# A masked 4,096-key cross-attention: half of the mask moved from TensorE to a product on GpSimd

## The reference, cut to what matters

```python
energy = jnp.einsum('nqhd,nkhd->nhqk', q, k)
energy = jnp.where(mask == 0, jnp.float32(-1e+20), energy)
attn = jax.nn.softmax(energy / math.sqrt(EMBED), axis=3)
out = jnp.einsum('nhql,nlhd->nqhd', attn, v).reshape(N, q_len, HEADS * HEAD_DIM)
return out @ w_out.T + b_out
```

## Time and profile before

| what | us |
|---|---|
| median of 3 runs | 945.77 |
| the runs | 946.16, 945.77, 938.29 |
| span of the profiled execution | 937.9 |
| the run nearest to it | 938.29 |
| PE busy | 915.0 |
| DVE busy | 592.0 |
| ACT busy | 446.4 |
| POOL busy | 101.3 |

### The profile page before, as it was taken

How to read it: one execution, slowest core, us unless ns; L and a number is a source line. 1 busy time by engine, 2 the same in 40 slices (tenths; PEclk the granted TensorE clock), 3 DMA queues, 4 the chain that set the end, 5 groups by cost and what they waited for, 6 DMA issues and landing times.

```text
span 937.9 us, 20632 instructions
## 1 busy us (share of the span) xinstructions
PE 915.0 (98%) x7488; PEld 542.7 (58%) x7490; DVE 592.0 (63%) x1546; ACT 446.4 (48%) x835; POOL 101.3 (11%) x138
## 2 busy tenths in 40 slices
PE   8999999999999999899999999999999999999998
PEld 8888886557666556544444444444444444467656
DVE  3455445655332226777777877777777777558884
ACT  3444434541121224666666666666666666642110
POOL 1222221000600110100000000000000000003000
PEclk9999999999999999999999999999999999999999
DMA  7944598608117217993564455446545543710201
GB/s 252 298 171 168 178 384 286 201 2 272 57 31 118 79 48 197 280 211 63 69 85 71 61 77 81 66 61 83 75 62 71 83 65 82 137 45 1 46 24 45
DMA packets 78391, 109.88 MB, mean 117 GB/s; under 512 B 27036, under 2 KB 64544, under 8 KB 74307
## 3 DMA queue, kind: packets, MB, share of 16 engines
q1 hardware_dynamic: 73019, 93.70, 45.7%
q0 software_dynamic: 4960, 14.96, 4.3%
q10 hardware_dynamic: 360, 0.50, 0.2%
HBM read 86.29 MB, written 21.06 MB: 114 GB/s over the span
## 4 chain that ended last, share of the span: by engine, by line
PE 87%; DVE 5%; SPq 2%; DMA 2%; ACT 1%; issue 1%; ACTq 0%; POOL 0%; DVEq 0%
PE bank L1486 15%; PE bank L1507 13%; PE bank L1495 9%; PE bank L1464 7%; PE bank L1343 6%; PE bank L1137 5%; PE bank L1124 4%; PE bank L1371 3%; PE bank L1717 2%; PE bank L1090 2%; PE bank L1311 2%; PE bank L1229 1%; PE bank L1220 1%; PE bank L1777 1%; SPq L486 1%
## 5 line engine op out<-in xcount | busy, mean ns | idle before, releaser
L986 ACT ACTIVATE region<-bank 128x512 f32<-128x512 f32 x512 | 277.9, 595 | 152.0 <-PE bank L1495 152.0
L2192 DVE CUSTOM_DVE_ANT_0 xnT<-bank,region 128x1024 bf16<-128x1024 f32 x128 | 156.1, 1220 | 79.9 <-issue 79.8
L1486 PE MATMUL bank<-region 128*128 (+1 forms) x1024 | 158.1, 276 | 2.1 <-ACT region L986 1.4
L2192 DVE CUSTOM_DVE_ANT_0 region<-bank,region 128x1024 bf16<-128x1024 f32 x128 | 156.3, 1221 | 0.4
L1507 PE MATMUL bank<-region 128*32 128x256 f32 x2048 | 138.9, 385 | 0.0
L1486 PEld LDWEIGHTS bank<-region 128*128 128x128 bf16 x1024 | 69.5, 98 | 119.9 <-issue 59.8
L1495 PE MATMUL bank<-region,identb 64*64 64x512 bf16 x1024 | 105.2, 401 | 0.0
L1507 PEld LDWEIGHTS bank<-region 128*32 128x32 f32 x2048 | 58.9, 109 | 40.5 <-ACT region L986 14.5
L1464 PE MATMUL bank<-region,xnT 64*128 64x512 bf16 x248 | 75.1, 382 | 1.1 <-DVE region L2192 1.1
L1466 PE MATMUL bank<-region,xnT 64*128 64x512 bf16 x248 | 75.1, 382 | 0.0
L741 POOL COPY region<-region 128x512 f32<-128x512 f32 x30 | 18.4, 613 | 389.7 <-PE bank L1507 389.7
(11 more groups left out here) (384 smaller groups left out, 1228.1 us busy)
## 6 DMA issues: line engine op xcount, KB each, us to landing
region<-keys_split SPq DMA_DIRECT2D x224, 128.0 KB, 4.9
region<-in_ctx SPq DMA_DIRECT2D x32, 512.0 KB, 7.6
keys_split<-region POOLq DMA_DIRECT2D x48, 256.0 KB, 4.4
region<-in_L_ffn_we_gate SPq DMA_DIRECT2D x8, 688.0 KB
region<-in_L_ffn_we_up SPq DMA_DIRECT2D x8, 688.0 KB
region<-in_mask_1x1xSxS_ik SPq DMA_DIRECT2D x1, 4096.0 KB, 16.4
region<-in_L_ffn_we_down SPq DMA_DIRECT2D x8, 512.0 KB
mask_kept<-region SPq DMA_DIRECT2D x1, 2048.0 KB, 10.9
```

The source lines that it names most:

```text
L986: nc.scalar.activation(prob4[n % PROBS].rearrange("p a b -> p (a b)"), bank[:, SCORE4[n], :], ACT.Exp, scale=SCALE4).then_inc(exp4_ready, 1)
L1486: mm(bank[:, SCORE4[n], k * S:(k + 1) * S], slab[s][:, t * P:(t + 1) * P], qT4[:, bass.ds(u, 1), :].rearrange("p o q -> p (o q)"), start=( ...
L2192: v.tensor_tensor_reduce(out=junk[q], in0=bank[:, 3 + 2 * q:5 + 2 * q, :].rearrange("p a b -> p (a b)"), in1=maskN[:, q, 2 * c * CH:2 * (c ...
```

## The change

Of the eight groups of a unit, the even ones (POOLED = 0, 2, 4, 6) have no mask matmuls any more: their score4 is raised by the second score matmul. ACT takes the exponential of the unmasked scores. GpSimd then multiplies the 32 bits of each exponential, read as an integer, by an integer 0 or 1 (keep4), in place, one instruction of 128 x 512 for each half, so eight more in a unit, and raises probs_kept, for which values_group of these groups waits instead of exp4_ready. The copy of the values comes behind the second of the eight, and in the last unit the inverse root is in that place. The odd groups stay as they are; maskT holds only theirs.

keep4 is made in stage 2 by two ACT instructions per pooled group in place of one. The constant for masked becomes -2^67. Queries whose whole row is masked are handled apart: in stage 1 DVE also reduces each piece of the mask to its maximum (eight tensor_reduce) and, in chunks 11 to 14, subtracts the row's result (eight tensor_scalar); where a row is wholly masked, the variance of the norm before stage 4 is replaced by a huge one (floor in layer_stats, two small instructions changed). The mask's store to DRAM waits for chunk 14 instead of 10. wout and woutT lie in the first key slab, so wout is loaded when that slab has been used for the last time, behind unit 28's scores, ahead of the loads for stage 5 on SP, and its four transposes and ACT's copy stand in front of o4_T(0) in the last unit instead of behind stage 1.

```diff
+POOLED = (0, 2, 4, 6)
+ON_PE = [g for g in range(GROUPS) if g not in POOLED]
-MASKED = -float((np.float32(1e20).view(np.uint32) & np.uint32(0xFFFF0000)).view(np.float32))
+MASKED = -2.0 ** 67
...
-            sp.dma_start(wout[:, :, :], a["L1_xattn_w_out"].rearrange("(c p) n -> p c n", p=P)).then_inc(in_wout, 16)
...
+            sp.wait_ge(score4, HALVES * (U4 - RING + 1))
+            sp.dma_start(wout, a["L1_xattn_w_out"].rearrange("(c p) n -> p c n", p=P)).then_inc(in_wout, 16)
             sp.wait_ge(pool_done, H4)
...
-            for u in range(2, U4):
+            def next_values(u):
...
+            def keep_probs(u, k):
+
+                n = 2 * POOLED[k // 2] + k % 2
+                bits = prob4[n % PROBS].bitcast(I32)
+                pool.wait_ge(exp4_ready, HALVES * u + n + 1)
+                nc.gpsimd.tensor_tensor(out=bits, in0=bits, in1=keep4[k], op=ALU.mult).then_inc(probs_kept, 1)
+            pool.wait_ge(maskT_ready, GROUPS)
+            for u in range(U4):
+                for k in range(2 * len(POOLED)):
+                    keep_probs(u, k)
+                    if k == 1 and 1 <= u < U4 - 1:
+                        next_values(u + 1)
+                    elif k == 1 and u == U4 - 1:
+                        inverse_root(5, 0, QT)
...
+                if g in POOLED:
+                    for c in range(2):
+                        last = nc.scalar.activation(keep4[2 * POOLED.index(g) + c].rearrange("p a b -> p (a b)"),
+                                                    bf16_bank(3)[:, c * 2 * S:(c + 1) * 2 * S], ACT.Copy,
+                                                    scale=-1.0 / MASKED, bias=1.0)
...
+                    if n == 0 and last:
+                        wout_out()
                         o4T_out(0)
...
+                whole = n // 2 in POOLED
                 for k in range(2):
                     t = 2 * n + k
...
+                              start=(k == 0), stop=whole, skip_group_check=True)
+                if whole:
+                    last.then_inc(score4, 1)
...
-                pe.wait_ge(exp4_ready, HALVES * u + 2 * g + 2)
+                if g in POOLED:
+                    pe.wait_ge(probs_kept, 2 * len(POOLED) * u + 2 * POOLED.index(g) + 2)
+                else:
+                    pe.wait_ge(exp4_ready, HALVES * u + 2 * g + 2)
...
-                    score_mask(g)
+                    if g not in POOLED:
+                        score_mask(g)
...
+                    link(v.tensor_scalar(part, mask_raw[:, q, k * 1024:(k + 1) * 1024], 0.0, MASKED, ALU.is_equal, ALU.mult))
+                    v.tensor_reduce(seen[:, q, k:k + 1], part, AX.X, ALU.max)
...
+                        last = v.tensor_scalar(part, part, all_masked[:, q:q + 1], None, ALU.subtract)
```

More of the change, by code:

```diff
@@ L76 @@
 NEG4 = 1
+WOUT4 = 5
 KT4 = CTX // P
@@ L259, in build @@
         mask_raw = A2.take([QT, CTX], I32)
-        maskT = Arena(region, mask_at, shared_at).take([KT4, S], BF16)
+        A1 = Arena(region, mask_at, shared_at)
+        maskT = A1.take([4 * len(ON_PE), S], BF16)
+        keep4 = [A1.take([2, S], I32) for n in range(4)]
+        A1 = Arena(region, spare_at, total)
+        keep4 += [A1.take([2, S], I32) for n in range(4)]
         maskN_made = Arena(region, slot_at(7), tail_at).take([QT, CTX], BF16)
@@ L297, in build @@
         hT3 = A1.take([FT, P])
-        A1 = Arena(region, both, total)
+        A1 = Arena(region, both, spare_at)
         silu = [A1.take([T]) for s in range(2)]
@@ L306, in build @@
         got3 = Arena(region, A1.at - 2 * CTX, A1.at).take([TOP, TT, D])
-        A1 = Arena(region, slot_at(2), total)
+        A1 = Arena(region, shared_at, shared_at + 2 * CTX)
+        wout, woutT = A1.take([DC, D]), A1.take([DC, D])
+        A1 = Arena(region, slot_at(2), spare_at)
         ctx_nat = [A1.take([KT4, D])]
@@ L847, in mask_out @@
                 act.wait_ge(maskT_psum, g + 1)
-                nc.scalar.activation(maskT[:, 4 * g:4 * g + 4, :].rearrange("p a b -> p (a b)"), bf16_bank(3),
-                                     ACT.Copy).then_inc(maskT_ready, 1)
+                if g in POOLED:
[4 more added lines that the diff above has]
+                else:
+                    t = 4 * ON_PE.index(g)
+                    last = nc.scalar.activation(maskT[:, t:t + 4, :].rearrange("p a b -> p (a b)"), bf16_bank(3), ACT.Copy)
+                last.then_inc(maskT_ready, 1)
             def values_out(g):
@@ L1160, in _ @@
                 turn1(1, i, i < TURNS1 - 1)
-            pe.wait_ge(mask_ready, QT)
-            pe.wait_ge(identb_ready, 1)
+            pe.wait_ge(mask_ready, 2)
             pe.wait_ge(x_added1, TURNS1 + 1)
-            pe.wait_ge(in_wout, 16)
-            for c in range(DC):
-                for o in range(DC):
-                    last = nc.tensor.transpose(bank[:, 4 + c, o * P:(o + 1) * P], wout[:, o, c * P:(c + 1) * P], ident[:, :])
-            last.then_inc(wout_psum, 1)
             pe.wait_ge(in_w2, 16 * N_W2)
@@ L1564, in unit, with wout_T @@
                         between(j, True)
+            def wout_T():
+                pe.wait_ge(in_wout, 32)
+                for c in range(DC):
+                    for o in range(DC):
+                        last = nc.tensor.transpose(bank[:, WOUT4 + c, o * P:(o + 1) * P], wout[:, o, c * P:(c + 1) * P],
+                                                   ident[:, :])
+                last.then_inc(wout_psum, 1)
             def o4_T(b):
@@ L1853, in _, with layer_stats @@
             link = Link(dve, dve_link)
-            def layer_stats(ts):
+            def layer_stats(ts, floor=None):
                 for t in ts:
@@ L1940, in mask_step @@
                 if 3 <= c < 11:
-                    q, k = (c - 3) // 4, (c - 3) % 4 * 1024
-                    last = v.tensor_scalar(maskN_made[:, q, k:k + 1024], mask_raw[:, q, k:k + 1024], 0.0, MASKED,
-                                           ALU.is_equal, ALU.mult)
-                    if k == 3 * 1024:
-                        last.then_inc(mask_ready, 1)
+                    q, k = (c - 3) // 4, (c - 3) % 4
+                    part = maskN_made[:, q, k * 1024:(k + 1) * 1024]
+                    link(v.tensor_scalar(part, mask_raw[:, q, k * 1024:(k + 1) * 1024], 0.0, MASKED, ALU.is_equal, ALU.mult))
+                    v.tensor_reduce(seen[:, q, k:k + 1], part, AX.X, ALU.max)
+                if c == 11:
+                    link(v.memset(small[0:1, 3:4], 0.0))
+                    link(v.tensor_reduce(all_masked[:, :], seen[:, :, :], AX.X, ALU.max))
+                    v.tensor_scalar(no_query[:, :], all_masked[:, :], HUGE_VAR / MASKED, None, ALU.mult)
+                if 11 <= c < 15:
+                    for q in range(QT):
+                        part = maskN_made[:, q, (c - 11) * 1024:(c - 10) * 1024]
+                        last = v.tensor_scalar(part, part, all_masked[:, q:q + 1], None, ALU.subtract)
+                if c == 14:
+                    last.then_inc(mask_ready, 1)
             def turn1(b, i):
@@ L2175, in _ @@
                 split_queries(t)
-            layer_stats(halves[1])
+            layer_stats(halves[1], no_query[:, :])
             def later_scale():
```

54 lines of the change are left out of this document (31 added, 23 removed).

## The result

The changed kernel took 910.89 us (median of 4 runs, 906.76 to 919.07) against 945.96 us before: a ratio of 0.965, 95% interval 0.958 to 0.972. Run again beside the later experiments it gave 909.36 us (6 runs), ratio 0.963 (0.960 to 0.967). Predicted were 910 us and a range of 895 to 940. The runs of one kernel spread by some 12 us with TensorE's mean granted clock (0.987 to 0.998 in those of after); the kernel before was profiled at 0.998, so where a stage is compared in microseconds I take beside the first profile of after (span 917.4 us, clock 0.987) the second one (span 907.0 us, clock 0.998).

The account below looks back on a forecast made before the run. TensorE was taken as the bound, at 13.64 us per unit. Units 1 to 30 -30.6, unit 31 -1.1, first unit +1.0, wout +0.6, stage 2 +0.3: -29.8, 937.9 to 908.1 us; given as 910, range 895 to 940.

Parts of the forecast that it names:

- A mask is worth 0.34 us: Stage 4, TensorE: each group's mask matmuls removed save 0.34 us, four per unit 1.36, from 13.64 to 12.28 us.
- the ring: Closed chain through VectorE across the unit's start, from turning the negated maximum; takes back 0.34 us, leaving 12.6 per unit.
- the second pair: Second pair of maxima in a unit's first turn: TensorE may start it only after VectorE's maximum 1, 0.34 us late.
- Rival 3: Stage 4: the ring through VectorE has slack, so 12.28 us per unit, 10 us more gain, 898 us; chance 0.10.
- rival 4: Stage 4, TensorE: the change-over of tiles comes back, 4 x 0.11 us per unit, +14, 922 us; chance 0.08.
- The price of a product: GpSimd, stage 4: 1.155 us per product, busy 9.85 of 12.6 us; GpSimd becomes the bound from 1.50 us.
- POOL beside DVE: Stage 4: products and maxima don't hinder each other; products pass between VectorE's tiny instructions with 0.1 us to spare; nothing charged.
- rival 2: VectorE's small instructions wait for products: 13.8 us per unit, 941 us, or 923 with half the units hit; chance 0.12.
- First unit: +1.0: Stage 4's first unit: products queued behind the late context's copies cost +1.7 us, less 0.7 for two masks.
- Last unit and wout: -1.1 + 1.1 = 0: Last unit: -1.36 for masks, +0.3 for the root before products; +1.1 for wout's transposes and copy moved there.
- Before stage 4: -0.5 + 0.3: 0.5 us back from wout gone behind stage 1; +0.3 for stage 2's two half-size ACT copies instead of one.
- The sum: Whole kernel: terms total -29.8 us, 937.9 to 908.1; from the runs' median 945.77 it would be 916; 910 given.

Follow-up runs that it names:

- e11: e4 with four VectorE reductions in place of reduction, cast and subtraction of the negated maximum: 904.84 us, ratio 0.960.
- e1: The changed kernel without GpSimd's products, the values waiting for the exponentials alone: 907.34 us, ratio 0.960.
- e2: The changed kernel with only groups 2, 4 and 6 pooled, group 0's mask back on TensorE: 913.59 us, ratio 0.969.
- e6: The changed kernel with float32 products in place of int32 ones: 908.08 us, ratio 0.967.
- e17: The changed kernel with the four reductions of e11 and two of a unit's eight products done twice: 933.48 us, ratio 0.988.
- e3: The changed kernel with the odd groups 1, 3, 5, 7 pooled instead of the even ones: 941.70 us, ratio 0.998.
- e4: The changed kernel with groups 1, 2, 4, 6 pooled instead of the even ones: 944.24 us, ratio 1.000.
- e16: e11 with the first unit's copies behind two products and GpSimd waiting for VectorE's scaling in the last unit: 900.57 us, ratio 0.954.

## Why the prediction held, step by step

*A mask is worth 0.34 us.* Right. Where four paid masks go and nothing on the ring is blocked (e11), the unit falls from 13.64 to 12.34, 0.325 each.

*One of the four goes to the ring.* Right: the second pair is 0.30 us late, where 0.34 was forecast. e1 excludes the products as its cause, e2 shows that group 0's mask is free. The unit is 12.58 (forecast 12.6), over 30 intervals -32.7 us in the second profile (forecast -30.6 for units 1 to 30). Rival 3, a ring with slack, is out; so is rival 4.

*The price of a product.* Too low, without effect: 1.27 us by the row below, not 1.155, and in a unit GpSimd is busy 10.57, not 9.85.

```profile
L762 POOL TENSOR_TENSOR region<-region x256: 1262/1272/1466, 398.8 to 808.8; 128x512 int32<-128x512 int32 x128
```

e6 takes the type out as a reason; whether it is multiplying, working in place or the traffic beside it stays open. The bound stood where the sum put it: in e17 GpSimd sets the pace with 10 x 1.25 + 0.61. Eight leave 2 us of room. The Trainium skill's 2.6 cycles per element (GPSIMD Engine Reference, Performance versus the Vector engine), 1.1 us by the estimate, is 13% below what the trace shows.

*POOL beside DVE.* The forecast, that the products pass between VectorE's small instructions, is right for the even groups: cast 170 to 173 ns, subtraction 162 to 165 in all 32 units. But rival 2 is no idle one. The products ended at 609.43 and the cast began at 609.44, which is less even than the 0.1 us of room that I gave; behind the subtraction the room is 0.08 us. The gap was forecast, but with so little room it is in part luck that the even groups hit it. e3 and e4 move the products and lose everything, as the rival's 13.8 per unit had it (13.55 and 13.58). Of the two instructions, the subtraction has two SBUF inputs; the cast has one. The Trainium skill's rule (SBUF — State Buffer, Who interferes with whom) names a second class, instructions in a two-port mode, and the runs agree for cast and scaling, which were blocked, and for reductions, reciprocals and the maxima with one input in PSUM, which were not. I had priced only instructions on the ring and overlooked the scaling of the last unit, which is of the same class, and a multiplication of stage 5 with two inputs in SBUF that falls into that unit.

*First unit: +1.0.* Right in kind, too small. It went from 14.91 to 18.82 us in the first profile, and to 16.46, 15.36 and 18.99 with the same order in others, +0.5 to +4.1. In the first profile:

```profile
397.59 1.17 POOL L744 COPY region<-region 128x512 f32<-128x512 f32 x2 [13.94 <-DMA region<-in_ctx]
398.84 4.95 POOL L762 TENSOR_TENSOR region<-region 128x512 int32<-128x512 int32 x4
401.47 1.94 PE L1542 MATMUL bank<-region 128*32 128x256 f32 x16 [3.43 <-POOL region L762]
```

The queue behind the late context is as I said. From the copies' start to the first values it is 3.88 us here, and 3.89 in the second profile, where it was 1.83 before: +2.05 for a forecast of +1.7. Less the two masks that makes +1.35, near the +1.55 of the second profile. The rest of the spread is in good part TensorE's clock, for which I had charged nothing. Its stretches at half clock (0.50, the 1.2 GHz level), first in the kernel before, then in the first profile:

```profile
389.30:392.70 3.40, 3.25 (x18) 0.96 (x18) 2.25 (x5) 1.08 (x2) 0.09 (x1) 0.50 1.00 150
```

```profile
400.50:407.20 6.70, 5.73 (x36) 2.01 (x40) 2.21 (x5) 1.37 (x3) 5.78 (x5) 0.50 1.09 337
```

So the first unit of before has 3.4 us of it too, the second profile 3.4 (394.0 to 397.4), the first profile 6.8 (400.4 to 407.2), and e1, e2 and e16 none. At half clock half of the time is lost, so the first profile lost an estimated 1.7 us more there than the second. e1 (12.80) and e16 (13.88) are short by both, the shorter queue and the missing half clock; they show what can be had, but don't part the two. How late the context lands against the unit's start differs between profiles as well, and what decides on the half clock stays open.

*Last unit and wout: -1.1 + 1.1 = 0 from the last copy to the end.* Measured +3.4, in the second profile +1.8, without products -1.1 (e1). The products thus cost 2.9 to 4.5 us there instead of 0.3. In the second profile two blocked instructions of VectorE account for the 2.9. The scaling took 1.9 us longer. A multiplication of stage 5, under the last two products and on the chain that its running sums (L1725) wait for, took 1.1 longer; in the second profile and in e1:

```profile
798.60 1.50 DVE L2356 TENSOR_TENSOR region<-region 128x258 f32<-128x258 f32 x1
```

```profile
801.70 0.42 DVE L2352 TENSOR_TENSOR region<-region 128x258 f32<-128x258 f32 x1
```

It takes 1.50 us in e16 too, whose edit frees the scaling alone. The 1.6 us more of the first profile go with 3.4 us at half clock behind the scaling (799.9 to 803.3). For the root in front of the products, charged with 0.3, next to nothing is seen: there only a weight load waits for a product, 0.23 us. wout itself did as forecast: 0.50 us of transposes (787.48 to 787.98) and ACT's copy of 0.60.

*Before stage 4: -0.5 + 0.3.* TensorE began the first matmuls of stage 2 proper at 148.19 instead of 148.96. In the second profile the first copy is 1.6 us earlier, but 0.9 of that stand already at the end of stage 1's last matmuls (139.78 against 140.71), ahead of wout's place. In the first it is 4.9 later, because TensorE had half the clock in stage 2 (first row; the second is the same stretch in the second profile):

```profile
155.00:168.00 13.00, 13.00 (x46) 7.39 (x45) 6.44 (x12) 6.72 (x20) 0.00 (x0) 0.50 1.06 344
```

```profile
155.00:168.00 13.00, 12.41 (x82) 6.84 (x80) 9.37 (x19) 8.85 (x29) 0.00 (x0) 1.00 1.06 348
```

The changed kernel doesn't always bring it, as its second profile shows, and the kernel before, run again beside the experiments, had a mean clock of 0.987 to 1.000 and 950.3 to 938.2 us by it. *Stage 1* hid nearly all of VectorE's 18.4 us of extra work: with it, stage 1's last matmuls end 0.1 to 0.9 us earlier than before.

*The sum.* -29.8 forecast. In the second profile -1.6 + 1.6 - 32.7 + 1.8 = -30.9. Two errors met: the first and last unit cost 2.4 us more, and the units between and the stages before gave 3.5 us more than forecast. Between the medians the gain is 35 us. Runs of both kernels at clock 0.998 differ by some 33 us (938.3 to 942.6 before, 906.8 to 908.7 after); the rest is that more of the runs of before had a lower clock, and whether the change has a part in that stays open. I chose 910 between 908.1 and 916 without knowing the clock of the next runs, so that the median came within 1 us of it is luck; the range was not.

## What to carry to other kernels

Moving work to an idle engine is priced twice: by its own sum against the period, and by what it does to others' small instructions while it runs. Here eight products per unit gained 35 us or nothing, depending only on which groups they belong to. If tiny VectorE instructions stand on a ring, take forms that the neighbour cannot block (reductions, here) before tuning the timing, and look at the first and the last iteration by themselves.

## What the runs showed of the hardware

- A VectorE cast of 128 x 2 or subtraction of 128 x 2, 0.17 us alone, took up to 1.20 us while GpSimd multiplied (1.27 us per product), a multiplication of 128 x 32 went from 0.19 to 1.24, one of 128 x 258 from 0.42 to 1.50, and a tensor_scalar of 128 x 256 from 0.41 to 1.35 each; reductions of 128 x 2 stayed at 0.16.
- It goes the other way too: in e16 a product that began behind a VectorE addition of 128 x 1024 (777.08, 1.25 us) took 2.25 us.
- GpSimd's product of 128 x 512 takes 1.27 us in int32 and in float32; back to back they start 1.25 us apart.
- In the first profile of after a wait of 3.4 us on TensorE was followed by 5.7 us of work at clock 0.50; the kernel before had 3.4 us at that clock in its first unit without a wait for products.
